# Message passing on a hyperbolic ball: node additions dealt among other work, map words read at one place, and three one-hot tiles built by ScalarE

## The reference

```python
def _agg(entity_emb, relation_emb, head, tail, relation_type):
    head_emb = entity_emb[head]
    tail_emb = entity_emb[tail]
    rel_emb = relation_emb[relation_type]
    ricci = _l2_normalize(tail_emb + rel_emb)
    hyper_head = expmap0(head_emb)
    hyper_tail = expmap(tail_emb, hyper_head)
    hyper_rel = expmap(rel_emb, hyper_head)
    res = project(mobius_add(hyper_tail, hyper_rel))
    res = logmap(res, hyper_head) + ricci * 1e-07
    res = jax.nn.relu(res)
    sums = jnp.zeros(...).at[head].add(res)
    counts = jnp.zeros(...).at[head].add(1.0)
    return sums / jnp.clip(counts, 1.0, None)[:, None]
for _ in range(N_HOPS):          # N_HOPS = 2
    e = _l2_normalize(_agg(e, relation_emb, head, tail, relation_type))
    entity_res_emb = 0.5 * entity_res_emb + e
```

## Time and profile before

| what | value |
|---|---|
| time, median of 3 runs | 21005.64 us (20965.97 to 21025.58) |
| time of the profiled execution | 20999.39 us |
| its span, first to last instruction | 20997.5 us |
| DVE busy | 15524.9 us (74%) |
| POOL busy | 13093.3 us (62%) |
| PE busy | 9692.8 us (46%) |
| ACT busy | 2734.0 us (13%) |
| hop 1, from its first to its last DVE instruction | 14764.6 to 17789.8 us |
| hop 2, the same bounds | about 17909 to 20932 us |

### The profile page before, as it was taken

One profiled execution on the slowest core, in us unless ns is written; L12 is line 12 of the kernel. 1 busy time (PEld: TensorE's weight loads), 2 busy tenths in 40 slices (PEclk: granted clock), 3 DMA queues, 4 the chain that ended last, 5 costly groups with the idle time before them and its releaser, 6 DMA issues. The chain is left out here.

```text
span 20997.5 us, 207668 instructions
## 1 busy us (share of the span) xinstructions
PE 9692.8 (46%) x47565; PEld 6550.5 (31%) x47566; DVE 15524.9 (74%) x25713; ACT 2734.0 (13%) x6738; POOL 13093.3 (62%) x12678
## 2 busy tenths in 40 slices
PE   0333224655555555555777743332343433343443
PEld 0333222222222222222333333332333433343433
DVE  8555557999999999998888722222688887688887
ACT  0111100000000000000000000000233332233332
POOL 0788886666666666664777527774655653655653
PEclk9999996555555555555888855555555555555555
DMA  4333221111111111112111201114222222222222
GB/s 194 68 71 63 62 60 33 23 26 23 26 24 25 24 23 26 24 25 23 29 30 29 22 12 26 26 26 34 72 61 64 68 61 45 72 62 63 68 61 48
DMA packets 1151393, 956.47 MB, mean 46 GB/s; under 512 B 803963, under 2 KB 920315, under 8 KB 1150739
## 3 DMA queue, kind: packets, MB, share of 16 engines
q0 software_dynamic: 419904, 437.84, 12.3%
q1 hardware_dynamic: 730960, 512.22, 9.5%
HBM read 734.68 MB, written 210.63 MB: 45 GB/s over the span
## 5 line engine op out<-in xcount | busy, mean ns | idle before, releaser
L1539 POOL DMA_INDIRECT tail<-ball,h_idx x3328 | 3444.4, 1035 | 2802.9 <-DVEq L1864 1219.9
L809 PE MATMUL p_rad<-w_stack,hid_t 99*128 99x512 bf16 (+1 forms) x6656 | 2873.4, 588 | 2467.9 <-DVEq L908 1317.4
L1573 PE MATMUL h_sum<-head,h_hot 128*128 128x64 f32 x6656 | 1410.3, 410 | 3628.7 <-ACT head L1618 3273.9
L882 DVE TENSOR_REDUCE red<-prod 128x96 f32<-128x1536 f32 x1664 | 2904.0, 1745 | 3.5
L1573 PEld LDWEIGHTS h_sum<-head,h_hot 128*128 128x128 f32 x6656 | 1377.6, 320 | 3652.5 <-issue 3652.5
L345 POOL DMA_INDIRECT rec_a<-rec,slot x1600 | 2152.8, 1346 | 520.0 <-issue 492.6
L765 POOL DMA_INDIRECT rec_b<-l_rcb x1600 | 2077.2, 1298 | 570.6 <-issue 514.2
L1185 POOL DMA_INDIRECT l_xg<-h_tab,l_idx x1664 | 1570.0, 943 | 992.9 <-issue 492.3
L809 PEld LDWEIGHTS p_rad<-w_stack,hid_t 99*128 99x128 bf16 (+1 forms) x6656 | 776.3, 131 | 4215.2 <-issue 4159.3
L1007 POOL DMA_INDIRECT l_xg<-x_tab,l_idx x1664 | 1570.2, 944 | 662.2 <-issue 489.8
L743 POOL DMA_INDIRECT l_xg<-in_x,l_idx x1664 | 1577.7, 948 | 524.8 <-issue 475.5
(11 more groups left out here) (396 smaller groups left out, 18300.6 us busy)
## 6 DMA issues: line engine op xcount, KB each, us to landing
hot_t<-rows_l SPq DMA_DIRECT2D x208, 512.0 KB
rec_a<-fill SPq DMA_DIRECT2D x128, 728.0 KB, 19.6
l_rec<-rec_a SPq DMA_DIRECT2D x104, 896.0 KB, 4.8
rhot_t<-rows_r SPq DMA_DIRECT2D x208, 384.0 KB
tail<-ball,h_idx POOLq DMA_INDIRECT x3328, 2.5
t<-in_type SPq DMA_DIRECT2D x100, 500.0 KB
l_xg<-in_x,l_idx POOLq DMA_INDIRECT x1664, 2.4
l_xg<-x_tab,l_idx POOLq DMA_INDIRECT x1664, 2.4
```

Of the source, the lines that this page charges most:

```text
L809: ins = pe.matmul(p_rad[j % 3][:, h * 512:(h + 1) * 512], hid_t[j // 4 % 2][0:K3 + 3 * (1 - i), j % 4, i, :], w_stack[i][0:K3 + 3 * (1 - i ...
L882: ch.step(dve.tensor_reduce(red[:, j, :], prod[j % 3][:, :, :], AX, ALU.add))
L1539: pool.indirect_dma_start(tg[q][:, j, :], None, table[:, :], bass.IndirectOffsetOnAxis(ap=idx[q][:, j:j + 1], axis=0)).then_inc(gathered[q ...
L1573: ins = pe.matmul(p_sum[u % 2][:, j % BT // 2, :], hot[j // HP8 % 3][:, j % HP8, :], hg[:, j, 0:D], start=(j % 2 == 0), stop=(j % 2 == 1))
```

## The change

Four edits in `hop_phase`:

1. **Additions one at a time.** A new helper `apart` issues an instruction once all but the last of those ahead of it are done. In units 2 and 3 one addition stands behind each larger instruction (six of eight; two follow in a row). The eight of unit 2 stand among the eight instructions of `tails`, the eight of unit 3 among the instructions of `heads` for units 1 and 2. The wait for PE's sum stands at the head of the unit instead of behind it. In the last block, which has no `tails` and `heads`, units 2 and 3 are added as before.
2. **Map words.** PE reads all eight words of the next block at the head of the block's body, not two per unit. DVE reads its words where it did, but the second instruction of line 1858 now stands behind a wait.
3. **One-hots of half units 0, 1 and 2** are made by ACT: |lane - number| by Abs for each tile (8 instructions of 128 x 128), then 1 - that, clipped at zero, by one Relu of 128 x 1024. Half units 0 and 1 come behind the block's Tanh, half unit 2 behind its first Sqrt. For them DVE copies 24 columns of lanes to f32 (`h_lanes`) in `heads`.
4. The scratch `v2` is the third `h_hot` buffer, not the first.

```diff
 def body(b, q, it, left):            # PE
-    chunk = {}
+    chunk = {w: words(b + 1, w) for w in range(2 * HU)} if left else {}
     for u in range(HU):
-        if left:
-            for w in (u, u + HU):
-                chunk[w] = words(b + 1, w)
         hold(pe, turn, added, b * HU + (u + 1))
...
+def hots(b, m):                      # ACT
+    for j in range(HP8):
+        ins = act.activation(hot[m][:, j, :], g["row"][:, :], ACT.Abs, scale=-1.0, bias=lanes[:, m * HP8 + j:m * HP8 + j + 1])
+    ins.then_inc(away, 1)
+    hold(act, turn, away, b * 3 + (m + 1))
+    act.activation(hot[m][:, :, :], hot[m][:, :, :], ACT.Relu, scale=-1.0, bias=one[:, 0:1]).then_inc(edge_hot, 1)
+
 def body(b, q, it, left):
     hold(act, turn, asked, b * (5 + HU) + 1)
     act.activation(sc[:, T:T + 2, :], sc[:, NORM:NORM + 2, :], ACT.Tanh).then_inc(told, 1)
+    hots(b, 0)
+    hots(b, 1)
     hold(act, turn, asked, b * (5 + HU) + 2)
     act.activation(sc[:, ROOTS:ROOTS + 2, :], sc[:, ROOTS_IN:ROOTS_IN + 2, :], ACT.Sqrt).then_inc(told, 1)
+    hots(b, 2)
     hold(act, turn, asked, b * (5 + HU) + 3)
...
+def apart(f, *a, **k):               # DVE
+    if ch.n > 1:
+        dve.wait_ge(chain_s, ch.n - 1)
+    ch.step(f(*a, **k))
+
+def between(add, u):
+    if add is None:
+        ch.sync()
+    else:
+        add(u)
+
+def with_relation(vec, out, u, add, k):
+    apart(tt, v2[:, :, 0:NREL3], vec[:, unit(u), T_REL:T_REL + NREL3], rhot[:, unit(u), :], MUL_)
+    between(add, k)
+    apart(dve.tensor_reduce, out[:, unit(u)], v2[:, :, 0:NREL3], AX, ADD)
+    between(add, k + 1)
...
 for u in range(HU):
     z = unit(u)
-    for vec, c in ((h, 16), (t, 18)):
-        ch.step(tt(vec[:, z, 0:D], vec[:, z, 0:D], bc(sc[:, c, z].unsqueeze(2), big), MUL_))
+    add = adder(u - 2) if u >= 2 else None
+    if u >= 2:
+        add(None)
+    apart(tt, h[:, z, 0:D], h[:, z, 0:D], bc(sc[:, 16, z].unsqueeze(2), big), MUL_)
+    if u >= 2:
+        add(0)
+    apart(tt, t[:, z, 0:D], t[:, z, 0:D], bc(sc[:, 18, z].unsqueeze(2), big), MUL_)
     load_chunks()
-    ch.sync()
-    ch.step(tt(h[:, z, 0:D], h[:, z, 0:D], t[:, z, 0:D], ADD))
+    between(add, 1)
+    apart(tt, h[:, z, 0:D], h[:, z, 0:D], t[:, z, 0:D], ADD)
     load_chunks()
-    ch.sync()
+    between(add, 2)
...
-    for m in range(2):
+    for m in range(max(3 - 2 * u, 0), 2) if u else ():
         hots(q, b, 2 * u + m)
+        between(add, 4 + m)
...
     if u >= 2:
-        add_unit(u - 2)
+        add_rest(u - 2, 6)
 dve.sem_inc(ends_used, 1)
 if left:
     compares(b + 1, 3)
-add_unit(2)
-add_unit(3)
-if left:
-    tails(1 - q, it + q)
-    heads(1 - q, b + 1)
+    adder(2)(None)
+    tails(1 - q, it + q, adder(2))
+    dve.sem_inc(added, 1)
+    heads(1 - q, b + 1, adder(3))
+    dve.sem_inc(added, 1)
+else:
+    for u in (2, 3):
+        adder(u)(None)
+        add_rest(u, 0)
```

More of the change, by code:

```diff
@@ L1470, in hop_phase @@
         rhot_t = [sb(f"rhot_t{k}" + tag, [3 * NREL3, BT, P], BF16) for k in range(3)]
-        v2 = hot[0][:, :, :].rearrange("p t (a d) -> p (t a) d", d=D)
+        v2 = hot[2][:, :, :].rearrange("p t (a d) -> p (t a) d", d=D)
         sc = sb("sc" + tag, [P, 38, W])
+        lanes = sb("h_lanes" + tag, [P, 3 * HP8])
+        one = sb("h_one" + tag, [P, 1])
         p_head = [ps(f"h_head{k}" + tag, [P, 4, P]) for k in range(3)]
@@ L1636, in _ @@
             ch = Chain(dve, chain_s)
-            ch.do(dve.memset(acc[:, :, :], 0.0))
+            ch.step(dve.memset(acc[:, :, :], 0.0))
+            ch.step(dve.memset(one[:, :], 1.0))
+            ch.sync()
             ch.restart()
@@ L1663, in hots @@
                 z = slice(m * HP8, m * HP8 + HP8)
[L1664 to L1667, removed]
+                dve.wait_ge(sum_done, b * (2 * HU) + (m - 2))
+                apart(tt, hot[m % 3][:, :, :], lane3, bc(ends[q][:, 0, z].unsqueeze(2), [P, HP8, P]), ALU.is_equal)
             def relation_hots(q, it):
@@ L1687, in heads @@
                     z = unit(u)
+                    mine = add if u in (1, 2) else None
+                    k = 4 * (u - 1)
                     dve.wait_ge(taken, b * Q + ((u + 1) * H + 1))
-                    with_relation(hg, sc[:, HV + 1, :], u)
-                    ch.do(tt(v2[:, :, :], hg[:, z, 0:D], t[:, z, 0:D], MUL_))
-                    ch.do(dve.tensor_reduce(sc[:, HV, z], v2[:, :, :], AX, ADD))
+                    if u == 1 and add is not None:
+                        add(None)
+                    with_relation(hg, sc[:, HV + 1, :], u, mine, k)
+                    apart(tt, v2[:, :, :], hg[:, z, 0:D], t[:, z, 0:D], MUL_)
+                    between(mine, k + 2)
+                    apart(dve.tensor_reduce, sc[:, HV, z], v2[:, :, :], AX, ADD)
+                    between(mine, k + 3)
                 dve.wait_ge(rel_taken, b * Q + (Q + 2))
@@ L1696, in heads @@
                 ch.step(dve.tensor_copy(sc[:, VV + 1, :], rg[:, :, D]))
+                ch.step(dve.tensor_copy(lanes[:, :], ends[q][:, 0, 0:3 * HP8]))
                 ch.sync()
@@ L1847, in load_chunks, with adder, add, add_rest @@
                     chunk.extend(chunks(dve, g["map"][1], b * (N2 // PACK) + len(chunk) // PACK))
-                def add_unit(u):
-                    dve.wait_ge(sum_done, b * (2 * HU) + (2 * u + 2))
-                    add_groups(dve, ch, chunk[u * BG:u * BG + BG], acc, lambda k: p_sum[u % 2][:, k:k + 1, :])
+                def adder(u):
+                    def add(k):
+                        if k is None:
+                            dve.wait_ge(sum_done, b * (2 * HU) + (2 * u + 2))
+                            return
+                        at = acc[:, bass.ds(chunk[u * BG + k], 1), :]
+                        apart(tt, at, at, p_sum[u % 2][:, k:k + 1, :], ADD)
+                    return add
+                def add_rest(u, first):
+                    ch.sync()
+                    for k in range(first, BG):
+                        adder(u)(k)
+                        ch.sync()
                     dve.sem_inc(added, 1)
```

28 lines of the change are left out of this document (18 added, 10 removed).

## The result

| | before | after |
|---|---|---|
| time, median of 4 runs each | 20992.87 us | 20309.33 us (20296.32 to 20325.25) |
| ratio | | 0.9674, 95% interval 0.9657 to 0.9691 |
| span of the profiled execution | 20997.5 us | 20323.4 us |

The changed kernel takes 683.5 us less, 3.3%. Forecast were 20255 us, a range of 20090 to 20520, and 0.96 for faster: right, and 54 us too low.

A forecast was written before the change was run, and what follows sets the result against it. DVE was taken as the bound, PE behind it in a block's second half. Blocks 14.9 us shorter give 745 us, last blocks 10: 755 off 20999.4, run median 6 higher: 20250; near misses make it 20255, range 20090 to 20520.

The forecast's parts named there:

- two waits on sum 0: DVE waits for PE's first sum: 1.4 us ahead of half unit 3, 2.1 us at the head of unit 2.
- rival A: Each of 28 dealt additions costs its full 0.22 us, not 0.04: 252 us more, 20510 us; chance 0.10.
- 0.5 us for the words: In units 2 and 3 the addition stands behind DVE's map word too, delaying the next large instruction 0.5 us.
- 0.3 us on units 0 and 1: DVE's second scaling waits, so its first map word starts later and the next large instruction starts at 2.7, not 2.4.
- The step of 9.7 us: PE's distance from sum to sum falls from 11.6 to 9.7 us once map words leave its path.
- rival B: PE's faster clock falls on sums, so DVE's waits of 1.4 and 2.1 us shrink: 175 us, 20080 us; chance 0.07.
- rival C: Gathers on POOL become the bound if DVE's denser work stretches each by 0.25 us: 20500 us; chance 0.04.
- ACT's part: ACT's one-hot work between Tanh and Sqrt takes 7.1 us within 14.8 us of idle time, costing nothing.
- Rival D: Slower: DVE waits at `told` for ACT's one-hots, at 1.8 us for each Abs: 21075 us; chance 0.02.

The follow-up runs named there:

- only_hots: Kernel before with only ACT making the first three half units' one-hots, plus the rewriting's helpers, against the kernel before: 21021.70 us, ratio 1.0022.
- hots_undone: Changed kernel with DVE making all one-hots again, against the changed kernel rerun on the same third chip: 24299.27 us, +16 us.
- only_words: Kernel before with only PE reading all map words at the block's head, plus the rewriting's helpers, against the kernel before: 20883.99 us, ratio 0.9956.

## Why the prediction was right

**The bound and the exchange.** DVE bounds the hops with PE behind it in the second half of a block: right. The step that carries the result, that two waits on sum 0 would take up what the one-hots free (t = 12.7 and 16.2), is in the trace at 12.8 and 16.2, and `only_hots` (+40 us, where the helpers by themselves cost 39 on the second chip) and `hots_undone` (+16) show how little is left of the 4.1 us.

**Additions.** Taken at 0.04 us each, rival A at 0.22. In `heads` they are free: units at 4.05 us with and without four of them. In `tails` a product with its reduction and two additions takes 15770.67 - 15769.15 = 1.52 us, 0.04 for each addition, since it took 1.44 without. The second product of `tails` before, beside the first in the earlier trace rows:

```profile
15750.82 0.69 DVE L1675 TENSOR_TENSOR h_hot<-tail,h_rhot 128x512 f32<-128x512 f32 x1
```

So 0.04 is high for `heads` and right for `tails`. In units 2 and 3 it was too low. From one-hot to one-hot it is 15754.87 - 15753.41 = 1.46 with an addition and was 1.37, 0.09. Between the two scalings an addition costs 0.14 us (15748.58 - 15747.30 = 1.28, before 1.14), and behind the second scaling, where the sequencer also reads a map word, the step grew from 1.26 to 1.69 us. The prediction had put most of that apart, as 0.5 us for the words. The queued PSUM operand, which no row of before showed, behaves as the queued scalings. The Trainium skill, page "VectorE: DVE Perf Modes", section "The DRAIN you can't avoid", has the next instruction wait until the flush is over, but adds that one which isn't held starts earlier; the prediction used only the first half for rival A, and these rows are the second. The addition at 15769.76 starts 0.61 us behind a product that lasts 0.69, and the reduction starts 0.13 behind that addition, which lasts 0.21. Rival A is out.

**Map words on DVE.** Here a step was wrong. The prediction said that the second scaling waits for the first, and put 0.3 us on units 0 and 1. `apart` leaves the last instruction out of the wait, so the two still start 1.14 us apart (15731.08, 15732.22), and units 0 and 1 take 5.4 us as before. It cost the forecast little, for the wait behind them took up the 0.6 us: it is 2.16 and not 1.4 us, and the next is 2.19 where 2.1 was forecast. Only where an addition stands between the scalings does the word delay the next one, in units 2 and 3: 9.95 us each where 9.8 were forecast.

**PE.** The gaps went: 337.7 to 6.2 us. The step of 9.7 us was not how it went on. In the 3 us windows of the block's second sum PE was granted 0.75 and 1.00 of its clock (1.00 is 2.4 GHz), against 0.50, 1.2 GHz, in the first sum. Windows with the columns of the earlier trace rows, then PE's timeline, its first row from the block ahead of the one shown:

```profile
15743.00:15746.00 3.00, 3.00 (x16) 0.50 0.23 53
...
15749.00:15752.00 3.00, 3.00 (x28) 0.75 0.18 41
...
15752.00:15755.00 3.00, 3.00 (x48) 1.00 0.18 36
...
15646.30 7.07 PE L1572 MATMUL h_sum<-head,h_hot 128*128 128x64 f32 x32
...
15749.52 4.23 PE L1572 MATMUL h_sum<-head,h_hot 128*128 128x64 f32 x32
...
15757.65 7.06 PE L1572 MATMUL h_sum<-head,h_hot 128*128 128x64 f32 x32 [2.59 <-DVEq L1893]
...
15767.47 3.80 PE L1572 MATMUL h_sum<-head,h_hot 128*128 128x64 f32 x32 [0.32 <-issue]
```

The second sum took 4.23 us instead of 7.06, the last one 3.80. The block shown stands for about half of them: the second sum took 3.76 to 4.30 us in 28 of the 52 blocks and 7.07 in the others, as in the block ahead (15646.30, also without a gap in front), where a later sum was the fast one. The first sum took 7.06 us in all 52. The fast stretches are rival B's mechanism, and the prediction had read the rows at 0.50 against it. By the Trainium skill, page "TensorE: Matmul & The Clock Gate", section "What's actually happening", activity releases the throttle. The trace agrees in that the clock rose where PE had been busy without a gap, or behind one of 0.32 us ahead of the last sum. It differs in that six blocks, the one ahead among them, had three sums of 7.06 to 7.07 us in a row without a gap before the clock rose. The fast stretches brought no time. In the block shown PE then stood 2.59 us for the additions of unit 0, and DVE's two waits hang on the first sum, which the clock did not change. The block ahead, with its second sum at 7.07 us, took 100.60 us (from 15592.38 to 15692.98), and one with its second sum at 3.83 us took 100.55 (from 15392.62 to 15493.17). I had not listed `added` among the waits at all. In the changed kernel it stands where PE has slack; in `only_words`, which brought 98 us of the 275 expected, it was PE's largest wait but for the one ahead of a block's first sum.

**Gathers, and ACT.** POOL's gathers took 1047 ns on the mean after 1035, 0.012 us more each where rival C needed 0.25: it is out. ACT's part took 7.2 us between Tanh and the next wait where 7.1 were forecast, and 8.27 us of idle time remained ahead of the Sqrt:

```profile
15698.65 2.43 ACT L1604 ACTIVATE h_hot<-row,h_lanes 128x128 f32<-128x128 f32 x8
...
15701.20 1.15 ACT L1607 ACTIVATE h_hot<-h_hot,h_one 128x1024 f32<-128x1024 f32 x1
...
15714.23 1.28 ACT L1615 ACT_TABLE_LOAD   x1 [8.27 <-DVEq L1811]
```

Rival D is out by that.

**The size.** The block was forecast at 97.0 us, and at 98.7 with the loop's turn in the mean; the one shown took 97.5, and the means are 99.6 and 99.75. In the block shown the two units of 9.95 instead of 9.8 us make 0.3 of the 0.5 (the second ends at 15767.20, where `compares` begin), `tails` 0.1, and from `heads` to the next block it is 52.9 for 52.8. The prediction's own sum has two slips here that nearly cancel: its parts of a unit add up to 9.9 us and not 9.8, and 37.8 + 5.8 + 0.3 is 43.9, where it has `heads` begin at 44.2. Its range, said to take in rival B, ends just above it: 20080 is below 20090.

The rest of the error is in the means. At the turn of the loop DVE stands still for "issue", 3.46 and 1.91 us in the turn shown (15692.98, 15695.43). In hop 1 this row grew from 34.5 to 55.3 us, 0.8 us a block. Against it stands a gain that the prediction did not have: in the last but one block of a hop DVE had waited for the rows of `rhot_t`, and in hop 1 that wait went, 0.4 us a block. Before, hop 1; after, hop 1 and hop 2:

```profile
17603.43 0.75 DVE L1656 TENSOR_SCALAR hot_t<-hot_t,lane 128x2048 bf16<-128x2048 bf16 x1 [11.25 <-DMA rhot_t<-rows_r]
...
17292.68 0.83 DVE L1667 TENSOR_SCALAR hot_t<-hot_t,lane 128x2048 bf16<-128x2048 bf16 x1 [0.50 <-DMA rhot_t<-rows_r]
...
20087.83 0.75 DVE L1667 TENSOR_SCALAR hot_t<-hot_t,lane 128x2048 bf16<-128x2048 bf16 x1 [11.17 <-DMA rhot_t<-rows_r]
```

So hop 1's 99.6 us are 98.7 + 0.5 + 0.8 - 0.4, and the 11 us that this wait gave are luck. In hop 2, whose code is the same, neither happened: the turn took 34.3 us before and 35.9 after, in 11 times each, and the wait for rows 10.68 and 11.17 us. Its mean lies 1.05 us above the forecast, of which the block shown explains 0.5. Why the second stall comes in hop 1 alone, why the rows came in time only there, and where hop 2 loses the other 0.5 us, stays open: no run tests it.

## What to carry to other kernels

An instruction taken off the busiest engine brings nothing if the engine then meets a wait whose end another engine sets; find who holds that end (here a Relu behind 32 small scalings) and move it: that brought 124 us where the one-hots by themselves had brought nothing. That the saved instructions then become worth something is likely but not shown, since the two runs that would tell were made on different chips. Small dependent instructions on VectorE, 0.35 us each in a row here, cost 0 to 0.14 us each when they were dealt one by one behind larger ones and waited only for the one before last, and more where the sequencer had other work at that place. When a double buffer lies between two engines, price the wait for its release in both directions: making one side faster alone ends at that wait.

## What the runs showed of the hardware

- An addition of 128x64 queued behind a larger instruction on VectorE cost 0 to 0.14 us, also with an operand in PSUM, where each of a row of waited-for ones cost 0.35. Beside a map word that the sequencer read, the step grew by 0.43 us.
- TensorE's granted clock rose to 1.00 within f32 sums where PE had run without a gap (4.23 us instead of 7.06) or behind one of 0.32 us (3.80), and was back at 0.50 in the sum behind a gap of 2.59 us. Which sum was the first fast one differed: the second in 28 of 52 blocks, never the first.
- The changed kernel took 20309 us on one chip and 24284 on another, with PE idle for "issue" ahead of its sums for 6 us in the hops on the one and 2013 on the other. The change was worth 3.3% on the one and 2.6% on the other, and which of the two chips a kernel ran on mattered some six times more.
